# Block 0's groups in another order, its loads and stores moved, and the last block's quantised rows made by VectorE

## The chip, the cores and the metric

The kernel runs on the 8 cores of one Trainium2 chip. Each core computes 4 of the 32 sequences and shares nothing with the others. The time is the device time of the slowest core, in microseconds. Three runs of the kernel before took 1630.64, 1654.71 and 1867.44 us, so their median is 1654.71 us.

## What is computed

For each of 32 sequences of 2048 rows of 1024 numbers, one layer:

```
xn  = layernorm(x)
qkv = xn @ w_in.T                           # 1024 -> 3 x 1024, 16 heads of 64
o   = sliding window attention(q, k, v)     # blocks of 512 queries; each looks at its own
                                            # block and the one before, bias slope*distance
a   = o @ w_out.T
s   = max(max|xn| of the row, 1e-6) / 127   # the quantised branch
xq  = clip(round(xn / s), -128, 127)        # whole numbers
f   = (xq @ weight_q.T) * s * weight_scale + bias
out = x + a + f
```

## The kernel before

**Blocks, slots, steps.** A core handles 16 blocks of 512 rows (t = 0 to 15), four to a sequence; four row chunks (tc = 0 to 3) of 128 make a block. The program is unrolled in Python: for each block 8 slots (one per pair of heads) of 5 steps (one per tile of the attention matrix). A step is written (slot, i). In each step TensorE gets, in this order, the scores of one tile (L805, or L828 for slots 3 to 7), at most one *group* of 8 matmuls of 128x512 (L645, function `group`), and `pv`, probabilities times V, of earlier tiles (L897). The first block of a sequence has no previous block, so its slots have four tiles of 512, 384, 256 and 128 columns and an empty fifth step.

**The groups.** `K p` and `Q p` make keys and queries of head pair p, `V h tc` values of half h, `F tc h` is the quantised product, `P tc h` the output projection. `K+`, `Q+`, `V+` belong to the next block. `PLAN` says which group goes into which step; block 0 has its own table, `PLAN_0`, as it has no block before it whose F and P it could compute. The last block's remaining F and P follow in `LAST_SLOT` and `END_PLAN`. Groups write two PSUM banks (`dn`) in turn, so a group waits until the copy out of the group two before it is done.

**The chain of a slot.** When the last `pv` of a head pair is done, `den` (L910 to L913, ScalarE, three instructions) makes the reciprocal of the row sums at step 2 of the next slot (step 1 after an odd pair of 3 or more), `norm` (L920, L923, VectorE) multiplies at the step after it, and only then may `pv` of the next pair, at step 4, write the same two banks `oa` and `ob`. Masks (L881) are VectorE's too.

**Rows of x.** `xn_load`, `xn_stat`, `xn_norm`, `xn_amax` take the next block's rows: load by SyncE, statistics (L474 to L477) and maximum (L535) by VectorE, the rest by GpSimd; `xn_turn_dma` turns the four chunks by DMA (TN). They use two buffers `xpre`, so chunks 2 and 3 are loaded when chunks 0 and 1 are finished with. For block 1 the tables `SECOND_*` say at which steps of block 0 this happens.

**Quantised rows.** `xr_load` loads x again, `xq_make` quantises a chunk by six GpSimd instructions (L610, L614, L617, twice) into the single buffer `xq`, `xq_turn` turns it by DMA into one of two `xqfm`, `xq_bias` adds the bias to x on GpSimd (L628, four instructions), and `add_rows` (L737) adds that to u. For the last block `LAST_LOAD`, `LAST_MAKE`, `LAST_TURN` and `LAST_BIAS` give the steps.

**Weights.** They lie in DRAM as float32 and are cast by GpSimd's DMA queue. The K and Q weights of block 0 (numbers 0 to 15) come first and lie where `wq` and `wout` go later (`wq_sb`: 0 to 7, `wout_sb`: 8 to 15). Numbers 16 to 31 (block 1's) pass through four buffers `wqk` in turn and are stored as bf16 in DRAM (`w2bf`, by SyncE's queue, `store_wqk`); number n + 4 is loaded from float32 only after number n is stored. From number 32 on, SyncE loads them from `w2bf`. Each engine, and each of the two queues that issue DMAs (SyncE, GpSimd), works in the order written.

## Time and profile before

| | us |
|---|---|
| three runs | 1630.64, 1654.71, 1867.44 |
| the profiled execution, its own time | 1626.06 |
| its span on core 7, the slowest | 1624.4 |
| spans of the 8 cores | 1612.8 to 1624.4 |
| TensorE busy | 1576.1 (97%) |
| ScalarE, VectorE, GpSimd busy | 1058.5, 937.5, 840.8 |

The span runs from the first to the last instruction of a core, the profiled execution's own time is 1.66 us more. All times below are us from the span's start. In a row of a timeline "x8" counts merged instructions, and the bracket says how long the engine sat idle before the row and what released it.

### The profile page before, as it was taken

Reading aid. Unit: us, or ns where it says so; the run is one execution under the profiler, and the core shown is the slowest. Engines: PE = TensorE matmul, PEld = TensorE weight load, DVE = VectorE, ACT = ScalarE, POOL = GpSimd, SP = SyncE. Lnnn points to the kernel's source line nnn. Section 1 sums busy time; section 2 is a strip of 40 time slices with the busy share of each in tenths; the row PEclk is TensorE's granted clock in tenths of the full one; section 3 lists DMA queues with packets and bytes.
Section 4 is the critical chain, followed back from the end, with each engine's and each line's share of the span. In section 5 each row is a group of like instructions: output and inputs, shape, how many; then the busy total and the mean of one; then the engine's idle time right before and its main releaser. Section 6 shows DMA issues by size and latency. Waiting matters only on the chain.

```text
span 1624.4 us, 29492 instructions; the slowest of 8 cores (1612.8 to 1624.4 us)
## 1 busy us (share of the span) xinstructions
PE 1576.1 (97%) x8736; PEld 747.4 (46%) x8736; DVE 937.5 (58%) x1699; ACT 1058.5 (65%) x1966; POOL 840.8 (52%) x1258
## 2 busy tenths in 40 slices
PE   5788999999999999999999999999999999999997
PEld 2334444454444445444444544445444444544443
DVE  3644647556474665646556574655747566565453
ACT  4564776767656676776754667677675666767662
POOL 6325545535564564545546553464536645464275
PEclk9999999999999999999999999999999999999999
DMA  8948643635446353443535445343453634435232
GB/s 157 234 103 201 160 121 104 175 92 137 134 119 177 105 144 111 133 133 105 147 120 152 134 119 148 112 129 120 122 153 109 175 106 132 135 105 164 78 81 82
DMA packets 208705, 213.96 MB, mean 132 GB/s; under 512 B 139932, under 2 KB 140060, under 8 KB 208040
## 3 DMA queue, kind: packets, MB, share of 16 engines
q1 hardware_dynamic: 203368, 197.40, 42.9%
q0 software_dynamic: 5184, 14.68, 5.3%
q8 instruction: 76, 1.25, 0.3%
q14 instruction: 77, 0.63, 0.1%
HBM read 153.31 MB, written 37.75 MB: 118 GB/s over the span
## 4 chain that ended last, share of the span: by engine, by line
PE 88%; POOL 4%; DMA 4%; issue 1%; DVE 1%; ACT 1%; SPq 0%; POOLq 0%; DVEq 0%; ACTq 0%
PE dn L645 63%; PE oa L897 7%; PE ob L897 7%; PE sc L828 5%; PE sc L805 5%; DMA xqfm<-xq 1%; POOL xres L628 1%; DMA wv_sb<-wv 1%; DMA xpre<-x 1%; POOL u L737 1%; POOL xqt L610 1%; DMA xres<-x 1%; POOL xqt L614 1%; POOL xq L617 0%; POOL xpre L628 0%
## 5 line engine op out<-in xcount | busy, mean ns | idle before, releaser
L845 ACT ACTIVATE p<-sc,kbias_sb 128x512 bf16<-128x512 f32 (+3 forms) x1120 | 493.2, 535 | 270.8 <-PE sc L828 203.9
L645 PE MATMUL dn<-xnfm,wqk 128*128 128x512 bf16 x1920 | 447.3, 379 | 0.5 <-DMA xnfm<-xn 0.5
L737 POOL TENSOR_TENSOR u<-u,xres 128x256 f32<-128x256 f32 x240 | 170.6, 731 | 269.7 <-DVE u L754 243.2
L881 DVE TENSOR_TENSOR p<-p,tri_sb 128x512 bf16<-128x512 bf16 (+1 forms) x608 | 254.6, 420 | 91.9 <-ACT p L862 85.3
L645 PEld LDWEIGHTS dn<-xnfm,wqk 128*128 128x128 bf16 x1920 | 179.7, 98 | 218.1 <-issue 19.2
L862 ACT ACTIVATE p<-sc 128x1024 bf16<-128x1024 f32 (+3 forms) x228 | 218.0, 956 | 86.5 <-PE sc L805 85.8
L645 PE MATMUL dn<-wq_sb,xqfm 128*128 128x512 bf16 x1024 | 245.4, 383 | 10.5 <-DMA xqfm<-xq 8.2
L645 PE MATMUL dn<-wv_sb,xnfm 128*128 128x512 bf16 x1024 | 241.9, 379 | 2.4 <-DMA wv_sb<-wv 2.4
L645 PE MATMUL dn<-wout_sb,ofm 128*128 128x512 bf16 x1024 | 241.7, 380 | 0.0
L897 PE MATMUL oa<-p,vst 128*128 128x256 bf16 (+3 forms) x896 | 219.6, 300 | 9.7 <-DVE ofm L923 8.8
L897 PE MATMUL ob<-p,vst 128*128 128x256 bf16 (+3 forms) x896 | 217.6, 299 | 0.0
L722 DVE SCALAR_TENSOR_TENSOR u<-dn,small,wsb_sb 128x512 f32<-128x512 f32 x124 | 93.1, 751 | 158.5 <-PE dn L645 155.8
L478 POOL TENSOR_SCALAR small<-small 128x1 f32<-128x1 f32 x60 | 11.4, 190 | 312.6 <-DVE small L477 302.9
L628 POOL TENSOR_TENSOR xres<-xres,biasb_sb 128x256 f32<-128x256 f32 x248 | 167.0, 705 | 0.0
L754 DVE TENSOR_TENSOR u<-dn,u 128x512 f32<-128x512 f32 x124 | 85.7, 691 | 136.0 <-PE dn L645 131.0
L645 PEld LDWEIGHTS dn<-wq_sb,xqfm 128*128 128x128 bf16 x1024 | 97.8, 98 | 127.3 <-issue 22.7
L645 PEld LDWEIGHTS dn<-wv_sb,xnfm 128*128 128x128 bf16 x1024 | 100.0, 98 | 110.8 <-issue 4.0
L645 PEld LDWEIGHTS dn<-wout_sb,ofm 128*128 128x128 bf16 x1024 | 92.8, 98 | 119.7 <-issue 22.4
L920 DVE TENSOR_TENSOR ofm<-oa,r 64x512 bf16<-64x512 f32 x128 | 87.0, 680 | 98.7 <-ACT r L913 96.7
L897 PEld LDWEIGHTS oa<-p,vst 128*128 128x128 bf16 x896 | 87.8, 98 | 90.4 <-issue 11.6
L617 POOL TENSOR_SCALAR xq<-xqt 128x512 bf16<-128x512 f32 x128 | 79.7, 623 | 85.5 <-DMA xqfm<-xq 64.7
L910 ACT ACTIVATE r<-oa 64x512 f32<-64x512 f32 x128 | 76.1, 594 | 72.6 <-PE ob L897 70.0
(76 smaller groups left out, 1704.8 us busy)
## 6 DMA issues: line engine op xcount, KB each, us to landing
wqk<-w2bf SPq DMA_DIRECT2D x224, 256.0 KB, 2.9
xpre<-x SPq DMA_DIRECT2D x64, 512.0 KB, 4.4
xres<-x SPq DMA_DIRECT2D x64, 512.0 KB, 4.6
out<-u SPq DMA_DIRECT2D x124, 256.0 KB, 2.3
wqk<-w POOLq DMA_DIRECT2D x16, 256.0 KB, 6.9
w2bf<-wqk SPq DMA_DIRECT2D x16, 256.0 KB, 3.2
wq_sb<-w POOLq DMA_DIRECT2D x8, 256.0 KB, 11.2
wv_sb<-wv POOLq DMA_DIRECT2D x2, 1024.0 KB, 17.4
```

Of the source, the lines that this page charges most:

```text
L628: xb_ready[(t, tc)] = P.op("gpsimd", lambda e, cols=cols: e.tensor_tensor(out=buf[:, cols], in0=buf[:, cols], in1=biasb_sb[:, cols], op=AL ...
L645: tok = P.op("tensor", lambda e, k=k: e.matmul(out=dn[b][:, :], lhsT=lhs(k), rhs=rhs(k), start=(k == 0), stop=(k == n - 1)), waits=(waits ...
L722: v = P.op("vector", lambda e: e.scalar_tensor_tensor(out=u[:, :], in0=dn[b][:, :], scalar=xs[g][:, tc:tc + 1], in1=wsb_sb[:, cols], op0=A ...
L737: a = P.op("gpsimd", lambda e, q=q: e.tensor_tensor(out=u[:, 256 * q:256 * q + 256], in0=u[:, 256 * q:256 * q + 256], in1=buf[:, 512 * hal ...
L754: v = P.op("vector", lambda e: e.tensor_tensor(out=u[:, :], in0=dn[b][:, :], in1=u[:, :], op=ALU.add), waits=[tok, u_ready[(t, tc, half)]])
L805: tok = P.op("tensor", lambda e, h=h, slot=slot, tc=tc, c0=c0, c1=c1, hp=hp: e.matmul(out=sc[b % 2][:, 512 * hp + c0:512 * hp + c1], lhsT= ...
L828: tok = P.op("tensor", lambda e, r=r, slot=slot, tc=tc, c0=c0, c1=c1, hp=hp: e.matmul(out=sc[b % 2][:, 512 * hp + c0:512 * hp + c1], lhsT= ...
L845: tok = P.op("scalar", lambda e, c0=c0, c1=c1, hp=hp, o=o: e.activation(out=pbuf[b % NPB][:, 512 * hp + c0:512 * hp + c1], in_=sc[b % 2][: ...
L862: exp_done[b] = P.op("scalar", lambda e: e.activation(out=pt, in_=st, func=AF.Exp, scale=SCALE), waits=[sc_done[b]] + p_free[b % NPB])
L881: mask_done[b] = P.op("vector", lambda e: e.tensor_tensor(out=pt, in0=pt, in1=m, op=ALU.mult), waits=[exp_done[b], c_tok])
L897: end=end: e.matmul(out=bank[:, c0:c1], lhsT=vlhs(h, slot, tc), rhs=pbuf[bp % NPB][:, 512 * hp + c0:512 * hp + c1], start=(j == TILES[0]), ...
L920: P.op("vector", lambda e: e.tensor_tensor(out=dst[0:64, 512 * p:512 * (p + 1)], in0=oa[0:64, :], in1=r[0:64, :], op=ALU.mult), waits=[tok ...
```

## The change

It has three parts. **Block 0:** `PLAN_0` holds the same groups of slots 1 to 6 in other steps; chunks 2 and 3 of block 1's rows are loaded into `xres[1]` and `xres[2]` at steps (1, 0) and (1, 1), and their statistics, maxima and the turn come earlier; weights 2 and 3 are issued before the first rows' scalars and half 0 of V's weights one step sooner; `wq` is issued at (5, 1) instead of (3, 1) and waits for the turn of block 1's rows, `wout` at (7, 0) instead of (7, 2). **Stores:** numbers 16 to 19 are stored at (6, 0) of block 0, numbers 20 to 31 two at a time at step 2 of slots 0 to 5 of block 1; before, each K or Q group of number n issued the store of n + 2. **Last block:** `xq_make` is done by VectorE, four instructions to a chunk instead of six on GpSimd, from temporary tiles in `xn` into the free `xnfm`, and turned into `wv_sb`, whose weights are no longer needed; rows of chunks 2 and 3 are loaded into the other half of `wv_sb`, and load, make, turn and bias come earlier.

```diff
@@ -60,12 +60,12 @@
     [("V", 0, 1), ("V", 0, 2), ("V", 0, 3), None, None],
-    [("K", 2, 0), ("Q", 2, 0), ("V", 1, 0), None, None],
-    [("K", 3, 0), ("Q", 3, 0), ("V", 1, 1), None, None],
-    [("K", 4, 0), ("Q", 4, 0), ("V", 1, 2), None, None],
-    [("V", 1, 3), ("K", 5, 0), ("Q", 5, 0), None, None],
-    [("K", 6, 0), ("Q", 6, 0), None, None, None],
-    [("K", 7, 0), ("Q", 7, 0), None, None, None],
+    [None, ("K", 2, 0), ("Q", 2, 0), ("V", 1, 0), None],
+    [None, ("K", 3, 0), ("Q", 3, 0), ("V", 1, 1), None],
+    [("V", 1, 2), ("K", 4, 0), ("Q", 4, 0), ("V", 1, 3), None],
+    [None, ("K", 5, 0), ("Q", 5, 0), None, None],
+    [None, ("K", 6, 0), None, ("Q", 6, 0), None],
+    [None, ("K", 7, 0), ("Q", 7, 0), None, None],
     PLAN[7],
@@ -90,11 +90,10 @@
             (1, 4): ("P", 2, 1), (2, 0): ("P", 3, 0), (2, 1): ("P", 3, 1)}
-LAST_LOAD = {(0, 1): 0, (0, 2): 1, (5, 0): 2, (6, 3): 3}
-LAST_MAKE = {(4, 4): 0, (5, 3): 1, (6, 4): 2, (7, 2): 3}
-LAST_TURN = {(5, 2): 0, (6, 3): 1, (7, 2): 2, (7, 4): 3}
-LAST_BIAS = {(5, 2): 0, (6, 1): 1, (7, 1): 2}
-END_BIAS = (0, 0)
+LAST_LOAD = {(0, 1): 0, (0, 2): 1, (1, 3): 2, (1, 4): 3}
+LAST_MAKE = {(3, 4): 0, (4, 4): 1, (5, 4): 2, (6, 3): 3}
+LAST_TURN = {(4, 2): 0, (5, 2): 1, (6, 2): 2, (7, 1): 3}
+LAST_BIAS = {(4, 3): 0, (5, 2): 1, (6, 1): 2, (7, 1): 3}
@@ -103,10 +102,13 @@
 FIRST_SCALES = (1, 0)
-SECOND_LOAD = {(0, 3): 0, (0, 4): 1, (2, 3): 2, (3, 0): 3}
-SECOND_STAT = {(1, 4): 0, (2, 1): 1, (3, 3): 2, (4, 1): 3}
-SECOND_NORM = {(2, 0): 0, (2, 2): 1, (3, 4): 2, (4, 2): 3}
-SECOND_AMAX = {(2, 2): 0, (2, 4): 1, (4, 0): 2, (4, 4): 3}
+SECOND_LOAD = {(0, 3): 0, (0, 4): 1, (1, 0): 2, (1, 1): 3}
+SECOND_STAT = {(1, 4): 0, (2, 1): 1, (2, 4): 2, (3, 2): 3}
+SECOND_NORM = {(2, 0): 0, (2, 2): 1, (3, 0): 2, (3, 3): 3}
+SECOND_AMAX = {(2, 2): 0, (2, 4): 1, (3, 2): 2, (3, 4): 3}
+SECOND_TURN = (4, 1)
+
+STORE_STEP = 2
@@ -334,6 +336,7 @@
         wb_free = [[], []]
+        wv_free = [[], []]
         wqk_ready = {}
@@ -372,7 +375,9 @@
         def xsrc(t, tc):
-            return xpre[tc % 2] if t > 0 or tc < 2 else xres[tc - 2]
+            if tc < 2 or t > 1:
+                return xpre[tc % 2]
+            return xres[tc - 2 + t]
@@ -439,7 +444,7 @@
         g_half = P.op("gpsimd", lambda e: e.memset(mhalf[:, :], -0.5))
-        for seq in range(2):
+        for seq in range(4):
             load_first(seq, [xpre_ready[(0, 0)]])
@@ -456,7 +461,7 @@
         def load_wq():
-            late_w["wq"] = P.dma("gpsimd", wq_sb[:, :], wqh, "WQ", waits=wb_free[0])
+            late_w["wq"] = P.dma("gpsimd", wq_sb[:, :], wqh, "WQ", waits=wb_free[0] + xnfm_ready[1])
@@ -465,8 +470,11 @@
                 i = tc % 2
-                xpre_ready[(t, tc)] = P.dma("sync", xpre[i][:, :], xh[rows_of(t, tc), :], f"XP{i}",
-                                            waits=xpre_free[i])
+                if t == 1 and tc >= 2:
+                    sem, free = f"XR{tc - 1}", xres_free[tc - 1]
+                else:
+                    sem, free = f"XP{i}", xpre_free[i]
+                xpre_ready[(t, tc)] = P.dma("sync", xsrc(t, tc)[:, :], xh[rows_of(t, tc), :], sem, waits=free)
@@ -535,8 +543,8 @@
                 apply_absolute_value=True), waits=[stats[("d", t, tc)]])
-            if t == 0 and tc >= 2:
-                xres_free[tc - 2][:] = [tok, xn_ready[(t, tc)]]
+            if t <= 1 and tc >= 2:
+                xres_free[tc - 2 + t][:] = [tok, xn_ready[(t, tc)]]
             else:
@@ -594,16 +602,44 @@
-            if t == NT - 1 and tc < 2:
-                return xpre[tc], xpre_free[tc], f"XP{tc}"
-            i = (4 * t + (tc - 2 if t == NT - 1 else tc)) % NXR
+            if t == NT - 1:
+                if tc < 2:
+                    return xpre[tc], xpre_free[tc], f"XP{tc}"
+                return wv_sb[:, 2048 * (tc - 2):2048 * (tc - 1)].bitcast(F32), wv_free[0], f"XS{tc}"
+            i = (4 * t + tc) % NXR
             return xres[i], xres_free[i], f"XR{i}"
...
+        def xqfm_of(t, tc):
+
+            if t == NT - 1:
+                return wv_sb[:, 4096 + 1024 * tc:5120 + 1024 * tc], wv_free[1]
+            return xqfm[tc % 2][:, :], xqfm_free[tc % 2]
+
+        def xq_make_last(tc):
+
+            t = NT - 1
+            buf, g = xres_of(t, tc)[0], t % 3
+            for hf in range(2):
+                cols = slice(512 * hf, 512 * hf + 512)
+                tmp = xn[hf][:, :].bitcast(F32)
+                a = P.op("vector", lambda e, cols=cols, tmp=tmp: e.tensor_scalar(
+                    out=tmp, in0=buf[:, cols], scalar1=negm[g][:, tc:tc + 1],
+                    scalar2=alpha[g][:, tc:tc + 1], op0=ALU.add, op1=ALU.mult),
+                    waits=[xres_ready[(t, tc)], stats[("alpha", t)]] + xn_free[hf] + xnfm_free[NT % 2])
+                v = P.op("vector", lambda e, hf=hf, tmp=tmp: e.tensor_scalar(
+                    out=xnfm[NT % 2][:, 1024 * tc + 512 * hf:1024 * tc + 512 * hf + 512], in0=tmp,
+                    scalar1=MAGIC, scalar2=MAGIC, op0=ALU.add, op1=ALU.subtract), waits=[a])
+            xq_ready[(t, tc)] = v
+            stats[("taken", t, tc)] = a
+
         def xq_make(t, tc):
+            if t == NT - 1:
+                xq_make_last(tc)
+                return
             buf, g = xres_of(t, tc)[0], t % 3
@@ -630,9 +666,13 @@
         def xq_turn(t, tc):
-            dst = xqfm[tc % 2][:, :].rearrange("p (a b) -> p a b", a=8)
-            tok = P.turn(dst, xq[:, :], f"TQ{tc % 2}", [xq_ready[(t, tc)]] + xqfm_free[tc % 2])
-            xq_free[:] = [tok]
+            dst, free = xqfm_of(t, tc)
+            dst = dst.rearrange("p (a b) -> p a b", a=8)
+            src = xnfm[NT % 2][:, 1024 * tc:1024 * tc + 1024] if t == NT - 1 else xq[:, :]
+            tok = P.turn(dst, src, f"TL{tc}" if t == NT - 1 else f"TQ{tc % 2}",
+                         [xq_ready[(t, tc)]] + free)
+            if t < NT - 1:
+                xq_free[:] = [tok]
             xqfm_ready[(t, tc)] = tok
@@ -658,7 +698,6 @@
             xnfm_free[t % 2] = [tok]
-            store_wqk(seq + 2)
             if seq + 4 >= 32:
@@ -693,6 +732,7 @@
             xnfm_free[t % 2] = [tok]
+            wv_free[half][:] = [tok]
@@ -710,10 +750,12 @@
         def group_f(t, tc, half):
-            b, tok = group(8, lambda k: xqfm[tc % 2][:, 128 * k:128 * (k + 1)],
+            rows, free = xqfm_of(t, tc)
+            b, tok = group(8, lambda k: rows[:, 128 * k:128 * (k + 1)],
                            lambda k: wq_sb[:, 1024 * k + 512 * half:1024 * k + 512 * (half + 1)],
                            [xqfm_ready[(t, tc)], late_w["wq"]])
-            xqfm_free[tc % 2] = [tok]
+            if t < NT - 1:
+                free[:] = [tok]
             ui, u = u_of(t, tc, half)
@@ -970,7 +1012,7 @@
                         dense(t, LAST_SLOT[i] if t == NT - 1 and slot == 7 else (PLAN_0 if t == 0 else PLAN)[slot][i])
-                    if 0 < t + 1 < NT and at == XN_TURN_DMA:
+                    if 0 < t + 1 < NT and at == (SECOND_TURN if t == 0 else XN_TURN_DMA):
                         xn_turn_dma(t + 1)
@@ -988,12 +1030,11 @@
                     if t + 1 == 0:
+                        if at == (1, 3):
+                            load_wv0()
                         if at in FIRST_NORM:
...
                         if at == (1, 4):
-                            for seq in (2, 3):
-                                load_first(seq)
-                            load_wv0()
                             for seq in (4, 5):
@@ -1039,16 +1080,20 @@
                         xq_bias(t, LAST_BIAS[at])
-                    if t == NT and at == END_BIAS:
-                        xq_bias(t - 1, 3)
                     if t == 0 and at == (1, 0):
...
                             load_wqk(seq)
+                    if t == 0 and at == (6, 0):
+                        for seq in range(16, 20):
+                            store_wqk(seq)
+                    if t == 1 and slot < 6 and i == STORE_STEP:
+                        for seq in range(20 + 2 * slot, 22 + 2 * slot):
+                            store_wqk(seq)
                     if t == 0 and at == (2, 0):
                         load_late_constants()
-                    if t == 0 and at == (3, 1):
+                    if t == 0 and at == (5, 1):
                         load_wq()
-                    if t == 0 and at == (7, 2):
+                    if t == 0 and at == (7, 0):
                         load_wout()
```

How the order moves, first on TensorE in block 0. The piece of before begins with the second group of slot 1 (Q 2, step 1) and runs to slot 2's first scores (`sc`); `dn<-wv_sb` is V, `oa` and `ob` are `pv`.

```order
L645 MATMUL dn<-xnfm,wq_sb 128x512 x8
L805 MATMUL sc<-qa,ka 128x256
L805 MATMUL sc<-qb,kb 128x256
L645 MATMUL dn<-wv_sb,xnfm 128x512 x8
L805 MATMUL sc<-qa,ka 128x128
L805 MATMUL sc<-qb,kb 128x128
L897 MATMUL oa<-p,vst 128x512
L897 MATMUL ob<-p,vst 128x512
L897 MATMUL oa<-p,vst 128x384
L897 MATMUL ob<-p,vst 128x384
L805 MATMUL sc<-qa,ka 128x512
L805 MATMUL sc<-qb,kb 128x512
```

The change, from the first group of the same slot (K 2, now in step 1):

```order
L685 MATMUL dn<-xnfm,wq_sb 128x512 x8
L847 MATMUL sc<-qa,ka 128x256
L847 MATMUL sc<-qb,kb 128x256
L685 MATMUL dn<-xnfm,wq_sb 128x512 x8
L847 MATMUL sc<-qa,ka 128x128
L847 MATMUL sc<-qb,kb 128x128
L685 MATMUL dn<-wv_sb,xnfm 128x512 x8
L939 MATMUL oa<-p,vst 128x512
L939 MATMUL ob<-p,vst 128x512
L939 MATMUL oa<-p,vst 128x384
L939 MATMUL ob<-p,vst 128x384
L847 MATMUL sc<-qa,ka 128x512
```

K, Q and V each moved one step later: V now stands between the last scores of the slot and the `pv` that waits for `norm`, where no group stood, and none stands beside the scores of step 0.

SyncE's queue at the end of block 0, before. `WG0` to `WG3` are the loads of the four `wqk` buffers, from the turn of block 1's rows to the turn of block 0's first quantised chunk:

```order
L183 DMA_TRANSPOSE xnfm<-xn 128x8x128 [waits G] x2
L177 DMA w2bf<-wqk 128x1024 [waits WG0]
L177 DMA w2bf<-wqk 128x1024 [waits WG1]
L177 DMA w2bf<-wqk 128x1024 [waits WG2]
L177 DMA xres<-x 128x1024 [waits S]
L177 DMA w2bf<-wqk 128x1024 [waits WG3]
L177 DMA w2bf<-wqk 128x1024 [waits WG0]
L177 DMA w2bf<-wqk 128x1024 [waits WG1]
L183 DMA_TRANSPOSE xqfm<-xq 128x8x128 [waits G]
L177 DMA xres<-x 128x1024
```

The change, the same stretch:

```order
L185 DMA_TRANSPOSE xnfm<-xn 128x8x128 [waits G] x4
L179 DMA xres<-x 128x1024
L179 DMA w2bf<-wqk 128x1024 [waits WG0]
L179 DMA w2bf<-wqk 128x1024 [waits WG1]
L179 DMA w2bf<-wqk 128x1024 [waits WG2]
L179 DMA w2bf<-wqk 128x1024 [waits WG3]
L179 DMA xres<-x 128x1024 [waits V]
L185 DMA_TRANSPOSE xqfm<-xq 128x8x128 [waits G]
```

Two stores (numbers 20 and 21, the second `WG0` and `WG1`) no longer stand ahead of the turn `xqfm<-xq`, and the four others stand further from it.

VectorE in slot 3 of the last block, before (`u` is the copy out of an F or P group):

```order
L673 CAST k<-dn 128x512 [waits T]
L881 TENSOR_TENSOR p<-p,tri_sb 128x2x256 [waits S]
L673 CAST q<-dn 128x512 [waits T]
L881 TENSOR_TENSOR p<-p,tri_sb 128x2x128 [waits S]
L754 TENSOR_TENSOR u<-dn,u 128x512 [waits T,V]
L881 TENSOR_TENSOR p<-p,tri_sb 128x2x128 [waits S]
```

The change:

```order
L712 CAST k<-dn 128x512 [waits T]
L923 TENSOR_TENSOR p<-p,tri_sb 128x2x256 [waits S]
L629 TENSOR_SCALAR xn<-xpre,small 128x512 [waits XP0,TN]
L633 TENSOR_SCALAR xnfm<-xn 128x512 [waits V]
L629 TENSOR_SCALAR xn<-xpre,small 128x512
L633 TENSOR_SCALAR xnfm<-xn 128x512 [waits V]
L712 CAST q<-dn 128x512 [waits T]
L923 TENSOR_TENSOR p<-p,tri_sb 128x2x128 [waits S]
```

Four instructions (L629, L633, two halves) stand between a mask and the copy of Q out of PSUM; this happens in four slots. GpSimd's rows for them (24 in all) are gone.

## Rows read from the trace of the kernel before

**Rows 1.** The page, part 1: busy us, share of the span, instructions.
```profile
PE 1576.1 (97%) x8736; PEld 747.4 (46%) x8736; DVE 937.5 (58%) x1699; ACT 1058.5 (65%) x1966; POOL 840.8 (52%) x1258
```

**Rows 2.** Windows: length, busy of PE, PEld, DVE, ACT, POOL, clock, DMA, GB/s.
```profile
80.00:100.00 20.00, 14.52 (x64) 5.53 (x64) 9.70 (x21) 10.73 (x22) 1.49 (x2) 0.83 0.45 119
```

**Rows 3.** The chain that ended last, 0 to 165 us: start, us, what.
```profile
17.23 13.57 DMA wv_sb<-wv
...
114.87 17.51 DMA xqfm<-xq
```

**Rows 4.** Timeline of TensorE, block 0: start, us, line, operation, [idle before <- releaser].
```profile
31.18 1.89 PE L645 MATMUL dn<-wv_sb,xnfm 128*128 128x512 bf16 x8 [2.38 <-DMA wv_sb<-wv]
...
49.85 0.38 PE L897 MATMUL oa<-p,vst 128*128 128x512 bf16 x1 [2.19 <-DVE ofm L923]
...
51.04 3.48 PE L645 MATMUL dn<-xnfm,wq_sb 128*128 128x512 bf16 x8
...
60.71 0.38 PE L897 MATMUL oa<-p,vst 128*128 128x512 bf16 x1 [1.66 <-DVE ofm L923]
...
80.70 0.39 PE L828 MATMUL sc<-q,k 64*128 64x512 bf16 x2 [3.46 <-DVE q L673]
...
91.44 0.38 PE L897 MATMUL oa<-p,vst 128*128 128x512 bf16 x1 [3.36 <-DVE ofm L923]
...
93.24 3.02 PE L645 MATMUL dn<-xnfm,wout_sb 128*128 128x512 bf16 x8
...
100.35 0.39 PE L828 MATMUL sc<-q,k 64*128 64x512 bf16 x2 [1.76 <-ACT p L845]
...
101.44 1.89 PE L645 MATMUL dn<-xnfm,wqk 128*128 128x512 bf16 x8
```

**Rows 5.** Timeline of ScalarE and VectorE, block 0.
```profile
75.89 0.69 DVE L474 BATCH_NORM_STATS2 small<-xpre 128x6 f32<-128x512 f32 x1 [1.20 <-DMA xpre<-x]
...
86.07 1.78 ACT L845 ACTIVATE p<-sc,kbias_sb 128x384 bf16<-128x384 f32 x4 [3.08 <-PE sc L828]
...
87.88 0.59 ACT L910 ACTIVATE r<-oa 64x512 f32<-64x512 f32 x1
...
90.59 0.69 DVE L923 TENSOR_TENSOR ofm<-ob,r 64x512 bf16<-64x512 f32 x1
```

**Rows 6.** Timeline of TensorE, block 1.
```profile
119.16 1.89 PE L645 MATMUL dn<-xnfm,wqk 128*128 128x512 bf16 x8
...
132.93 3.57 PE L645 MATMUL dn<-wq_sb,xqfm 128*128 128x512 bf16 x8 [5.38 <-DMA xqfm<-xq]
```

**Rows 7.** Timeline of SyncE's queue and GpSimd, end of block 0.
```profile
85.12 29.66 SPq L177 DMA_DIRECT2D w2bf<-wqk  x3
...
108.79 0.62 POOL L617 TENSOR_SCALAR xq<-xqt 128x512 bf16<-128x512 f32 x1 [0.15 <-POOL xqt L614]
...
109.93 0.54 POOL L177 DMA_DIRECT2D wout_sb<-wout  x1
```

**Rows 8.** DMA issues, 0 to 170 us: count, KB each, us to landing.
```profile
wout_sb<-wout POOLq DMA_DIRECT2D x1, 2048.0 KB, 18.4
```

**Rows 9.** Timeline of TensorE, the end.
```profile
1592.24 1.89 PE L645 MATMUL dn<-wq_sb,xqfm 128*128 128x512 bf16 x8 [2.31 <-DVE p L881]
...
1600.80 5.29 PE L645 MATMUL dn<-wq_sb,xqfm 128*128 128x512 bf16 x16 [2.77 <-DMA xqfm<-xq]
...
1605.93 13.98 PE L645 MATMUL dn<-wout_sb,ofm 128*128 128x512 bf16 x64
```

**Rows 10.** Timeline of GpSimd and VectorE, the end.
```profile
1583.72 0.62 POOL L617 TENSOR_SCALAR xq<-xqt 128x512 bf16<-128x512 f32 x1 [2.28 <-DMA xqfm<-xq]
...
1590.80 0.75 DVE L722 SCALAR_TENSOR_TENSOR u<-dn,small,wsb_sb 128x512 f32<-128x512 f32 x1 [0.16 <-DMA out<-u]
```

**Rows 11.** Timeline of VectorE: two masks of one shape.
```profile
113.73 1.25 DVE L881 TENSOR_TENSOR p<-p,tri_sb 128x256 bf16<-128x256 bf16 x1 [2.38 <-ACT p L862]
...
121.88 0.42 DVE L881 TENSOR_TENSOR p<-p,tri_sb 128x512 bf16<-128x512 bf16 x1
```

2 lines of the change are left out of this document (1 added, 1 removed).

## The prediction

> **What bounds the kernel now.** I read the page's busy times first: TensorE works 1576.1 of 1624.4 us [rows 1], so it is the bound and a change can win only where it idles or runs slowly, 48 us in all. The page's slices put nearly all of that at the two ends. The engine's timeline says where. That of block 0, where a slot has only two or three groups, has six waits from 49.85 to 100.35: 2.19, 1.66, 1.63 (at 69.85, like the one before it and not shown), 3.46, 3.36 and 1.76, together 14.1 us [rows 4]. Four end at `norm`, one at the copy of Q 5, one at an exp. Ahead of them 2.38 us go to the first V weights. Three groups of 8 matmuls there last 3.48, 3.52 (at 81.79, not shown) and 3.02 us where 1.89 is normal (the row at 101.44): the windows row of 80 to 100 us has a granted clock of 0.83 [rows 2], so part of it ran at 1.2 instead of 2.4 GHz. Each such group comes behind one of the waits of 2.19 us or more; those of 1.66, 1.63 and 1.76 have none behind them. These three cost 1.6 + 1.6 + 1.1 = 4.3 us.
>
> In block 1 one wait is left: F 0 0 waits 5.38 us for its turned rows and then takes 3.57 us, 1.7 too long [rows 6]. SyncE's queue explains it: three stores held it from 85.12 to 114.78, because two of them wait for weights 20 and 21; only then, 5 us after the rows were made, was the turn issued, into the 2 MB load of `wout` that GpSimd had issued at 109.93 [rows 7]; it landed 17.51 us later [rows 3]. At the end [rows 9] TensorE waits 2.31 us for a bank, 2.77 us for the last turn, and 16 matmuls take 5.29 us instead of 3.5 (the row of 64 is 13.98, so 3.5 for 16). Behind both waits is GpSimd: its quantising waits 2.28 us for the buffer's turn, and the late copy out of F waits for a store of u that its queue had delayed [rows 10].
>
> **Block 0's order.** The count of groups stays, so TensorE's work does; only waits can change. Take the chain of slot 5: `den` starts at 87.88 and `norm` ends at 90.59 + 0.69 = 91.28, 3.4 us [rows 5]. Before, TensorE had K, Q and V in steps 0 to 2 and nothing beside `norm`. Now a slot of three groups has V (1.73 us, a 64-matmul row over 8) exactly there, and `pv` of the slot before comes one group sooner, so `den` may start sooner. For slots 1 to 3 I leave 0.4 us of waiting each, of 2.19 + 1.66 + 1.63. Slots 4 to 6 have two groups and nothing in step 3 except in slot 5. Counted from `pv`'s end: the exps of a tile or two (four instructions take 1.78, so 0.9 to 1.8) and the chain 3.4, less the two groups beside them, 3.5, leaves 0.8 to 1.7; with scores that must wait for their bank, I take 1.7 each. The wait for Q 5 was VectorE's: it stood at 75.89 for rows of x still landing [rows 5], behind which the copy of K 5 and `norm` queued. Those rows are now asked for some 20 us sooner, and the 2 MB of `wq` no longer compete. So the six waits fall from 14.1 to 1.2 + 5.0 = 6.2: **8 us won** (ends: 4, if the chain of each slot starts no sooner than now; 12, if nearly all close).
>
> **Clock in block 0.** With waits of 0.4 to 2 us I expect at most one slow group: 4.3 - 1.5, **3 us won** (0 to 4.3).
>
> **First V weights.** Before, the load was issued at 17.23 and took 13.57 us [rows 3]. Ahead of it now two issues less (0.54 each by the one of `wout` [rows 7]) and none of the last chunk's four scalars: 2.5 to 3 us sooner, with two weights out of its way. The scalars in turn slip a little, 0.2 us by my estimate. The wait of 2.38 goes: **2.2 us won** (0 to 2.4).
>
> **F 0 0.** Its turn has no store of numbers 20 and 21 ahead of it any more. K+ 0 was at 101.44 and F 0 0 due at 127.55; the quantised rows were ready at 108.79 + 0.62 = 109.4 [rows 7], so the turn is issued 18 us ahead of need, and even the 17.51 us of this time would do. **7.1 us won** (4 to 7.1). Late next could be weight 20: it stands in GpSimd's queue behind `wout`, now issued at the end of Q 7, 3.3 us before K+ 0. `wout` landed 18.4 us after its issue [rows 8], so 15.1 after K+ 0, weight 20 some 2 to 3 us later; it is due 119.16 - 101.44 = 17.7 us after K+ 0 [rows 4, 6]. So a wait of about **1 us** (0; 5 if `wq`, issued shortly before, still fills the queue, with 1.7 of slow clock).
>
> **The stores.** Twelve stores of 256 KB now come in pairs, each two steps before their buffer is loaded again. The loads they release are due 12 us and more later, so they cost nothing; the cover is that time, and without it a pair costs what the rival below says. Their bytes are the same.
>
> **The last block.** GpSimd loses 24 instructions of about 0.62 us [rows 10], 15 us, and no longer waits for one buffer. The bank comes free in time (2.31), the turn is ready (2.77), and the clock stays up (1.8). But P 0 0 needs `norm` of the last slot, which ends some 3.8 us after the last `pv`, the chain of 3.4 and its start; F 3 0 and F 3 1 fill 3.5, so 0.3 is left: **6.6 us won** (3 to 6.9). VectorE gains 16 `tensor_scalar` of 128x512. The trace has none of that size there. Bounds: 0.42, a bf16 mask of 128x512 [rows 11], and 0.75, the copy out of F [rows 10]; the operands are float32, but the pair reads one tensor, so I take 0.55. Four come in a row, 2.2 us, between a mask and the copy of Q. The copy is needed only two groups later (over 3.5 us), so the cover is the second bank and the masks' lead; I charge **1 us** in all (0 to 8). The upper end has its reason in a row: a mask of 128x256 took 1.25 us at 113.73, while GpSimd was adding, though twice the columns take 0.42 [rows 11]. If each of the four waits that long behind a bias or an add of GpSimd, a burst lasts 5 us.
>
> The Trainium skill (SBUF — State Buffer, Who interferes with whom) has a rule that speaks against moving this work: VectorE's two-input SBUF instructions and its 2-port modes share a port pair with GpSimd, and whoever comes second blocks fully. The slow mask agrees. By that rule, with every one of the 16 held up, the last block's term would be the upper end; without it, nothing.
>
> **Sum.** 8 + 3 + 2.2 + 7.1 - 1 + 6.6 - 1 = 24.9 us. The profiled execution took 1626.06, so 1601 us. The profile is 4.6 us under the lowest run shown (1630.64) and 29 under the median of the three, 1654.71, which the other two runs pull up; I put the time where most runs should be, **1603**.
>
> **The rivals.**
>
> *The chain keeps block 0* (0.20). A slot's waits only change places: ScalarE takes exps before `den`, and with two groups a slot is as long as its chain. For: the slot of K 6 and Q 6 already waited with only two groups. Against: in slots 1 to 3 TensorE idled exactly where V now stands. Then block 0 gives 4 + 0 instead of 8 + 3, and the time is 1603 + 7 = 1610.
>
> *VectorE becomes the hold-up of the last block* (0.12). Bursts of 5 us, as above, delay copies and masks four times by about 2 us: 1603 + 7, and if weight 20 is late as well, 1616. This is also the port rule's case. Against: VectorE is 58% busy and GpSimd has 15 us less to do.
>
> *Nearly all idle time goes* (0.16). Waits 12, clock 4.3, V 2.4, F 7.1, end 6.9 give 32.7, to 1593.
>
> *Slower than before* (0.04). Block 1's weights starve. A store stands behind everything that SyncE waits for; that queue has been held 29.66 us by three rows before [rows 7]. GpSimd then cannot reload its buffer and everything behind stands still, the quantising too. It decides from the point where a pair is held over 12 us. Held 17 us in each of the six slots, TensorE would wait 5 us and run slowly for 1.7, six times: 40 us, 1603 + 40 = 1643. Against it: no row ahead of these stores waits for anything that far off.
>
> *The forecast* (0.48). Everything above within a few us.
>
> **Numbers.** 1603. The range takes in the bounds: 1590 below; above, the two middle rivals and a run as far over the profile as those shown can be, 1630. Two per cent, about what a measurement of this kernel can tell from no change, is 32.5 us. Faster by more needs the third rival or an uneven pair of runs: 0.24. Within: 0.72. Slower: 0.04.
>
> **What would show it.** Right: `pv`'s waits for `norm` in block 0 at most 2 us each; K+ 0 at about 88 instead of 101.44; V's first group without a wait; no wait for `xqfm` anywhere; the last block's GpSimd share well down, and 64 matmuls of P starting some 4 us after the last `pv`. Wrong: waits of 2.5 us and over in slots 4 to 6 with groups of 3 us behind them; a wait of K 2 of block 1 for `wqk`; `tensor_scalar` rows of a microsecond and copies of Q that end late; new waits in block 1's slots. A run in which block 0 saves under 6 us would make the sum wrong by its largest term.

## The result: 1.2% faster, with 4 of the 11 us forecast for block 0

The changed kernel took 1608.47 us (median of 4 runs, 1607.27 to 1609.71). The kernel before took 1642.68 (median of 4 runs, 1626.28 to 1867.44). The ratios in this document leave out the disturbed runs, in which the cores of one die or both run at a lower granted clock; they are why the medians stand further apart. The ratio is 0.9884, with an interval of 0.9870 to 0.9898: faster by 1.2%, so under the 2% that count as a change here. The forecast was 1603 us, with 1590 to 1630 as its range. Its own sum said 24.9 us off the profiled execution's 1626.06; the new profiled execution took 1608.58, so 17.5 us went.

The page's busy times, to be read beside [rows 1]. TensorE's 1557.0 can't be compared to the us, since 167 of its matmul records are missing from this trace (8569 of 8736); idle times of 0.16 us "<-issue" are such holes.

```profile
PE 1557.0 (97%) x8569; PEld 746.1 (46%) x8736; DVE 949.3 (59%) x1715; ACT 1058.6 (66%) x1966; POOL 824.8 (51%) x1234
```

GpSimd has 24 instructions and 16.0 us less, VectorE 16 instructions and 11.8 us more.

Where the time went shows best if TensorE's timeline is cut at five instructions that both kernels have. In this table every figure is the mean over the eight cores, in us:

| stretch of TensorE's timeline | before | after | forecast |
|---|---|---|---|
| start to the first V group | 29.96 | 29.57 | -2.2 |
| first V group to K+ 0 | 67.26 | 63.28 | -11 |
| K+ 0 to the first `pv` behind F 0 0 | 35.15 | 28.62 | -6.1 |
| from there to the last `pv` | 1461.37 | 1459.76 | } -5.6 |
| last `pv` to P's 64 matmuls | 8.00 | 4.98 | } |
| P and the rest | 18.50 | 18.72 | 0 |
| span | 1620.25 | 1604.92 | -24.9 |

The mean span fell by 15.3 us, the slowest core's by 17.4 (1624.4 to 1607.0): the cores also lie closer together now, 1602.4 to 1607.0 instead of 1612.8 to 1624.4. I had read the stretches from core 7 of before, the slowest one. The fourth row also shows how far two mean spans can differ without a cause in the edit: in the runs below that change block 0 or its loads and stores (1, 3, 4, 6, 7, 8, 11, 12) it lies between 1458.2 and 1460.3.

TensorE's timeline in block 0 and the start of block 1, core 0, to be read against [rows 4, 6]: start, us, what, and in the bracket the idle time before it and its releaser.

```profile
46.00 0.38 PE L939 MATMUL oa<-p,vst 128*128 128x512 bf16 x1 [0.53 <-DVE ofm L965]
...
55.26 0.38 PE L939 MATMUL oa<-p,vst 128*128 128x512 bf16 x1 [1.34 <-DVE ofm L965]
...
66.53 0.38 PE L939 MATMUL oa<-p,vst 128*128 128x512 bf16 x1 [1.93 <-DVE ofm L965]
...
68.47 3.26 PE L685 MATMUL dn<-xnfm,wout_sb 128*128 128x512 bf16 x8
...
75.03 0.39 PE L870 MATMUL sc<-q,k 64*128 64x512 bf16 x2 [1.18 <-DVE q L712]
...
82.58 0.38 PE L939 MATMUL oa<-p,vst 128*128 128x512 bf16 x1 [1.00 <-DVE ofm L965]
...
90.95 0.39 PE L870 MATMUL sc<-q,k 64*128 64x512 bf16 x2 [2.32 <-DVE q L712]
...
92.35 3.27 PE L685 MATMUL dn<-xnfm,wqk 128*128 128x512 bf16 x8
...
119.88 1.89 PE L685 MATMUL dn<-wq_sb,xqfm 128*128 128x512 bf16 x8
```

The reader is to see three things. Three of the four waits for `norm` have shrunk, from 2.19, 1.66 and 3.36 to 0.53, 1.34 and 1.00; the third has grown from 1.63 to 1.93. The waits for a copy of Q have grown: 1.18 and 2.32 (2.4 and 2.32 on six of the eight cores) where there was one, of 3.46 on core 7 and 2.2 on core 0. And K+ 0 starts at 92.35 instead of the forecast 88 and is itself a slow group of 3.27; on the mean of the cores it went from 97.2 to 92.8. F 0 0 at 119.88 waits for nothing and lasts 1.89.

The granted clock of 80 to 100 us, 0.83 in [rows 2], is now 0.91 in the same window; core 0 of before had 0.83 there too (length, busy of PE, PEld, DVE, ACT, POOL, clock, DMA share, GB/s):

```profile
80.00:100.00 20.00, 16.41 (x79) 6.65 (x80) 8.87 (x20) 11.97 (x25) 3.75 (x6) 0.91 0.71 174
```

The end, TensorE's timeline, against [rows 9]:

```profile
1582.96 0.81 PE L939 MATMUL ob<-p,vst 128*128 128x384 bf16 x3
1583.61 3.62 PE L685 MATMUL dn<-wq_sb,wv_sb 128*128 128x512 bf16 x16
1588.26 13.97 PE L685 MATMUL dn<-wout_sb,ofm 128*128 128x512 bf16 x63 [1.04 <-DVE xn L764]
```

There is no wait for a bank and none for a turn, and 16 matmuls take 3.62 us instead of 5.29. The wait of 1.04, the same on all cores, ends at the copy of an F group out of PSUM. VectorE's rows that stand in GpSimd's place are shown in the last section.

### The profile page after: what moved, and what is told of

It is laid out like the page before. It is cut to its first block, busy times and chain, and to the rows that moved or that the text cites. A ratio compares the mean times of both kernels' runs of the same rounds, so it can differ in the third digit from the quotient of the medians.

```text
span 1607.0 us, 29298 instructions; the slowest of 8 cores (1602.4 to 1607.0 us)
## 1 busy us (share of the span) xinstructions
PE 1557.0 (97%) x8569; PEld 746.1 (46%) x8736; DVE 949.3 (59%) x1715; ACT 1058.6 (66%) x1966; POOL 824.8 (51%) x1234
## 4 chain that ended last, share of the span: by engine, by line
PE 89%; POOL 3%; issue 2%; DVE 1%; SPq 1%; DMA 1%; ACT 1%; POOLq 0%; DVEq 0%; ACTq 0%
PE dn L685 64%; PE ob L939 7%; PE oa L939 7%; PE sc L847 6%; PE sc L870 6%; SPq L185 1%; DMA xnfm<-xn 1%; POOL xres L664 1%; POOL u L779 1%; DMA xpre<-x 0%; DVE ofm L965 0%; POOL xqt L646 0%; ACT p L887 0%; SPq L179 0%; POOL xqt L650 0%
## 5 line engine op out<-in xcount | busy, mean ns | idle before, releaser
L923 DVE TENSOR_TENSOR p<-p,tri_sb 128x512 bf16<-128x512 bf16 (+1 forms) x608 | 258.2, 426 | 91.6 <-ACT p L904 81.5
L685 PE MATMUL dn<-wout_sb,ofm 128*128 128x512 bf16 x975 | 232.7, 380 | 7.4 <-issue 5.7
L685 PE MATMUL dn<-wq_sb,xqfm 128*128 128x512 bf16 x938 | 223.9, 379 | 2.2 <-issue 1.6
L939 PE MATMUL oa<-p,vst 128*128 128x384 bf16 (+3 forms) x881 | 214.1, 298 | 5.7 <-DVE ofm L965 4.8
L664 POOL TENSOR_TENSOR xres<-xres,biasb_sb 128x256 f32<-128x256 f32 x240 | 162.6, 709 | 0.0
L685 PEld LDWEIGHTS dn<-wq_sb,xqfm 128*128 128x128 bf16 x960 | 91.2, 98 | 106.8 <-issue 6.7
L870 PE MATMUL sc<-q,k 64*128 64x512 bf16 (+3 forms) x1120 | 112.5, 300 | 4.2 <-DVE q L712 3.5
L952 ACT ACTIVATE r<-oa 64x512 f32<-64x512 f32 x128 | 76.1, 594 | 61.4 <-PE ob L939 58.8
```

The source lines that it names most:

```text
L664: xb_ready[(t, tc)] = P.op("gpsimd", lambda e, cols=cols: e.tensor_tensor(out=buf[:, cols], in0=buf[:, cols], in1=biasb_sb[:, cols], op=AL ...
L685: tok = P.op("tensor", lambda e, k=k: e.matmul(out=dn[b][:, :], lhsT=lhs(k), rhs=rhs(k), start=(k == 0), stop=(k == n - 1)), waits=(waits ...
L870: tok = P.op("tensor", lambda e, r=r, slot=slot, tc=tc, c0=c0, c1=c1, hp=hp: e.matmul(out=sc[b % 2][:, 512 * hp + c0:512 * hp + c1], lhsT= ...
L923: mask_done[b] = P.op("vector", lambda e: e.tensor_tensor(out=pt, in0=pt, in1=m, op=ALU.mult), waits=[exp_done[b], c_tok])
L939: end=end: e.matmul(out=bank[:, c0:c1], lhsT=vlhs(h, slot, tc), rhs=pbuf[bp % NPB][:, 512 * hp + c0:512 * hp + c1], start=(j == TILES[0]), ...
```

## The experiments

All are edits of the changed kernel if nothing else is said. "Stretch" is the mean over the cores from the first V group to K+ 0. Spans by core come from the profiled execution.

**1. The old order of block 0's groups.**

```diff
-    [None, ("K", 2, 0), ("Q", 2, 0), ("V", 1, 0), None],
+    [("K", 2, 0), ("Q", 2, 0), ("V", 1, 0), None, None],
...
```

> The changed kernel (ratio 0.988 to the kernel before) with block 0's groups in their old steps; loads, stores, statistics and the last block stay changed. Theory A (the chain of a slot bounds block 0, and the new order of groups hides a part of it): `pv` waits for `norm` again 1.6 to 2.2 us in slots 1 to 3, and the time from the first V group to K+ 0 of block 1, 63.3 us on the mean of 8 cores now and 67.3 before, comes to 67 or more; the ratio to before rises by 0.004 to 0.007, to 0.992 to 0.995. Theory B (block 0's gain came from the rows of x that land sooner, not from the order): the stretch stays at 63 to 64 us and the ratio at 0.988 to 0.990.

Ratio 0.9934 (0.9911 to 0.9957), as theory A has it. The stretch is 71.2 us against 63.3: the order wins 7.9 us here. But 71.2 is also 4.0 more than in the kernel before, which has this same order. In these stretches TensorE's mean idle time is 14.4 us (before 13.9, changed 10.5), its busy time for the same work 56.8 (53.3, 52.8), at a granted clock of 0.89 (0.95, 0.97). So half of the 7.9 is clock: behind waits of up to 3.4 us the groups ran partly at 1.2 GHz. The third wait for `norm` is 3.2 us here, twice that of before (1.63): the order is old, but the row statistics now stand ahead of it (run 6).

**2. The last block undone.** Rows quantised by GpSimd again, with the old steps:

```diff
-LAST_LOAD = {(0, 1): 0, (0, 2): 1, (1, 3): 2, (1, 4): 3}
-LAST_MAKE = {(3, 4): 0, (4, 4): 1, (5, 4): 2, (6, 3): 3}
+LAST_LOAD = {(0, 1): 0, (0, 2): 1, (5, 0): 2, (6, 3): 3}
+LAST_MAKE = {(4, 4): 0, (5, 3): 1, (6, 4): 2, (7, 2): 3}
...
```

> The changed kernel with the last block as it was: rows quantised by GpSimd at the old steps, one buffer xq, two xqfm. Theory A (GpSimd's quantising and its single buffer held up the end): the waits of some 2.3 us behind the last block's copies out of F and of 2.8 us for the last turn come back with a slow pair of groups; the time between the last `pv` and the first P group goes from 5.0 to 8 us on the mean of the cores, and the ratio rises by 0.003, to 0.991 to 0.992. Theory B (the bursts on VectorE cost as much as they save, the masks and copies they delay stall TensorE): no more than 0.001, 0.988 to 0.989.

Ratio 0.9927 (0.9912 to 0.9943). The mean span is 5.8 us longer, 2.8 of it between the last `pv` and P, where the wait for the last turn is back (2.8 us on seven cores), and 2.9 ahead of it, where the wait for a bank is back (1.7 to 2.5 us). The rest of the 2.9 is no more than that row's spread. Theory A holds; the forecast had 5.6 for this part.

**3. The old stores, `wq` and `wout`.** The stores of numbers 16 to 31 at the groups again, `wq` at (3, 1) without waiting for the turn of block 1's rows, `wout` at (7, 2):

```diff
+            store_wqk(seq + 2)
...
-                    if t == 0 and at == (5, 1):
+                    if t == 0 and at == (3, 1):
                         load_wq()
-                    if t == 0 and at == (7, 0):
+                    if t == 0 and at == (7, 2):
                         load_wout()
```

> The changed kernel with the stores issued by each K or Q group for the weights two ahead, wq issued at (3, 1) and wout at (7, 2), as before. Theory A (two stores ahead of the turn, and wout beside it, made F 0 0 wait): F 0 0 waits 4 to 6 us again and its group runs slowly, block 1's F 0 0 to K+ 0 distance goes from 28.5 back to some 35 us on the mean of the cores; ratio 0.992 to 0.993. Theory B (the turn is in time anyway since block 0 is shorter and the rows are ready): 0.988 to 0.989.

Ratio 1.0013 (0.9998 to 1.0029): all of the gain is gone. The stretch is 72.5 us, and the next one 35.3 as before: K+ 0 waits for its turned rows (up to 13.6 us) and F 0 0 for its own (2.6 to 6.3 us). The second is what theory A has; the first, which neither theory has, makes the loss more than twice as large as expected, and the kernel before has no such wait on any core. Three things are undone at once here; runs 7, 8 and 9 take them one by one.

**4. The old first weights.**

```diff
-        for seq in range(4):
+        for seq in range(2):
             load_first(seq, [xpre_ready[(0, 0)]])
...
```

> The changed kernel with the first weights issued as before: two ahead of the first rows' scalars, weights 2 and 3 and the first half of V's after them. Theory A (the two extra issues on GpSimd delay the first chunk's scalars by 1.5 us, which takes back most of what the earlier V weights give): first turn at 11.5 us instead of 13.0 and first K group at 19.6 instead of 20.5, but V's first group waits again 1.5 to 2.5 us and starts at 30 instead of 29.6; the ratio moves by less than 0.0005. Theory B (the first rows' delay is hidden behind the loads and the earlier V weights are worth 2.2 us): V's first group at 31.5 or later, ratio 0.0014 higher, 0.9898.

There is no ratio for this kernel; its two undisturbed runs took 1610.36 and 1612.35, and the spans are 1601.6 to 1608.7, mean 1604.81 against 1604.92. The first V group comes at 30.25 instead of 29.57, but the first transposes start at 11.66 instead of 13.04. By the mean span alone this part of the change would be worth nothing, but that difference is within the spread named above. Over all profiled kernels of this document the start of the first V group, as a mean over the cores, says more: with the first weights as changed it lies at 28.96 to 29.57 us (ten kernels, mean 29.2), with the old ones at 29.96 to 30.25 (the kernel before, runs 4 and 5, mean 30.2). So this part is worth about 1 us, and the changed kernel's own 29.57 is the latest of its ten. Theory A put the wait at 1.5 to 2.5 us; it is 1.3 on the mean and none to 2.6 by core.

**5. The kernel before with the new order alone.**

```diff
@@ kernel before @@
-    [("K", 2, 0), ("Q", 2, 0), ("V", 1, 0), None, None],
+    [None, ("K", 2, 0), ("Q", 2, 0), ("V", 1, 0), None],
...
```

> The kernel before with the new order of block 0's groups and nothing else. From the first V group to K+ 0 the kernel before takes 67.3 us on the mean of the cores, the changed kernel 63.3, the changed kernel with the old order 71.2. Theory A (the order is worth about 8 us wherever it stands, and the statistics of block 1's rows, moved earlier, cost block 0 about 4): this stretch takes 59 to 60 us, less than in the changed kernel, and the kernel is about 8 us below the kernel before, 0.995. Theory B (order and statistics only work together: the order pays because the rows come early and VectorE no longer waits for their load): the stretch takes 65 to 67 us, 0 to 2 us won, ratio 0.999. F 0 0 should wait 5 us or so in either case, since the stores are as before.

Ratio 0.9974 (0.9963 to 0.9985). The stretch is 63.9 us, 3.4 under the kernel before: between the theories, and nearer to B. The waits of TensorE on core 0 (engine, operation, what it waited for: us in total, times, longest) show what is left ahead of K+ 0, and that it is not what is left in the changed kernel; behind it F 0 0 waits 2.5 to 6.9 us, as both theories have it:

```profile
PE sc L828 <- DVE q L673: 5.8, 2, 3.4
PE dn L645 <- DMA wv_sb<-wv: 3.1, 1, 3.1
PE oa L897 <- DVE ofm L923: 3.1, 4, 1.3
```

The changed kernel, core 0:

```profile
PE oa L939 <- DVE ofm L965: 4.8, 4, 1.9
PE sc L870 <- DVE q L712: 3.5, 2, 2.3
```

With the rows of x late, VectorE stands for them and the copy of Q is late; with the rows early, their statistics run sooner, and `norm` is.

**6. The statistics behind `norm`.**

```diff
-SECOND_STAT = {(1, 4): 0, (2, 1): 1, (2, 4): 2, (3, 2): 3}
-SECOND_NORM = {(2, 0): 0, (2, 2): 1, (3, 0): 2, (3, 3): 3}
-SECOND_AMAX = {(2, 2): 0, (2, 4): 1, (3, 2): 2, (3, 4): 3}
+SECOND_STAT = {(1, 4): 0, (2, 0): 1, (2, 4): 2, (3, 0): 3}
+SECOND_NORM = {(2, 0): 0, (2, 2): 1, (3, 0): 2, (3, 2): 3}
+SECOND_AMAX = {(2, 3): 0, (3, 3): 1, (3, 4): 2, (4, 3): 3}
```

> The changed kernel; the statistics and the maxima of block 1's rows stand at other steps of block 0, none at steps 1 and 2, so that none lies ahead of the copy of Q and of norm. Theory A (VectorE's order in slots 2 and 3 lengthens the chain of a slot): the waits of pv for norm in slots 2 and 3, 1.34 and 1.93 us on core 0, fall under 0.7 together with the slow group behind them, the stretch from V to K+ 0 falls from 63.3 to 60 to 61.5, and the time is 2 to 3 us under that of the changed kernel. Theory B (the chain is den and ScalarE's exps; VectorE has slack): the stretch stays at 63 to 64. If the turn of block 1's rows then comes too late, K+ 0 would wait for xnfm, which neither expects: it is needed 14 us after the last row is made.

Ratio 0.9872 (0.9856 to 0.9888). The stretch falls from 63.3 to 61.3, the mean span from 1604.9 to 1601.6. VectorE's timeline of the changed kernel in slot 3 has the place:

```profile
60.98 0.69 DVE L712 CAST k<-dn 128x512 bf16<-128x512 f32 x1 [1.62 <-PE dn L685]
61.58 0.28 DVE L923 TENSOR_TENSOR p<-p,tri_sb 128x256 bf16<-128x256 bf16 x1
61.78 0.69 DVE L482 BATCH_NORM_STATS2 small<-xres 128x6 f32<-128x512 f32 x1
62.39 0.67 DVE L484 BATCH_NORM_STATS2 small<-xres 128x6 f32<-128x512 f32 x1
63.16 0.21 DVE L485 BATCH_NORM_AGGREGATE small<-small 128x2 f32<-128x12 f32 x1
63.29 1.19 DVE L543 TENSOR_REDUCE small<-xres 128x1 f32<-128x1024 f32 x1
64.40 0.68 DVE L712 CAST q<-dn 128x512 bf16<-128x512 f32 x1
65.00 0.67 DVE L962 TENSOR_TENSOR ofm<-oa,r 64x512 bf16<-64x512 f32 x1
65.69 0.69 DVE L965 TENSOR_TENSOR ofm<-ob,r 64x512 bf16<-64x512 f32 x1
```

Four instructions, 2.6 us, ahead of the copy of Q and `norm`; `norm` ends at 66.38 and TensorE's `pv` at 66.53 has waited 1.93. In the experiment the same place reads:

```profile
61.76 0.69 DVE L712 CAST q<-dn 128x512 bf16<-128x512 f32 x1 [0.84 <-PE dn L685]
62.37 0.67 DVE L962 TENSOR_TENSOR ofm<-oa,r 64x512 bf16<-64x512 f32 x1
63.05 0.69 DVE L965 TENSOR_TENSOR ofm<-ob,r 64x512 bf16<-64x512 f32 x1
```

and the `pv` behind it waits 0.24. On all cores the waits for `norm` in slots 1 to 3 are now 0.53, 0.40 and 0.25. The mean idle time in the stretch falls by 2.4 us (10.5 to 8.1), while the busy time grows by 0.4, at a granted clock of 0.96. Theory A holds.

**7. The old stores alone.** `store_wqk(seq + 2)` in the groups again; `wq` and `wout` as changed.

> The changed kernel with the stores of weights 16 to 31 where the kernel before has them; wq and wout stay at their new steps. Theory A (the stores alone made F 0 0 wait, as they held SyncE's queue ahead of the turn): F 0 0 waits 4 to 7 us, K+ 0 is not late, and the time is 5 to 8 us over the changed kernel. Theory B (it was the loads of wq and wout that filled the queues): F 0 0 does not wait and the time is that of the changed kernel within 1 us.

Ratio 0.9889 (0.9872 to 0.9907), that of the changed kernel. Theory A, that the stores alone made F 0 0 wait, falls. SyncE's and GpSimd's queues on core 0 (the `w2bf` row is read as in [rows 7]):

```profile
72.73 34.09 SPq L179 DMA_DIRECT2D w2bf<-wqk  x3
106.92 1.51 SPq L185 DMA_TRANSPOSE xqfm<-xq  x1
...
89.00 0.53 POOL L179 DMA_DIRECT2D wout_sb<-wout  x1 [16.45 <-PE dn L685]
```

The stores hold the queue even longer than before, 34.09 us, and the turn is issued at 106.92, 5.3 us later than in the changed kernel (101.67). But `wout`, issued at 89.00, had landed at 102.70 and no longer competes: GpSimd's next quantising, which waits for this turn, starts at 112.53, so the turn took at most 5.6 us and F 0 0 at 119.60 waits for nothing. On every core `wout` lands before this turn is issued, and the turn takes 4.5 to 6.0 us.

**8. `wq` early.**

```diff
-            ... "WQ", waits=wb_free[0] + xnfm_ready[1])
+            ... "WQ", waits=wb_free[0])
...
-                    if t == 0 and at == (5, 1):
+                    if t == 0 and at == (3, 1):
                         load_wq()
```

> The changed kernel with the load of wq two slots earlier and not waiting for the turn of block 1's rows; stores and wout as changed. Theory A (the turn and the 2 MB load must not be in flight together; the turn starves): K+ 0 waits for xnfm on most cores, up to 14 us, the stretch from V to K+ 0 is 70 to 73 us instead of 63.3, and F 0 0 does not wait. Theory B (the starving in the kernel with all of that undone came from its stores): the stretch stays at 63 to 64 and the time is that of the changed kernel.

Ratio 0.9957 (0.9912 to 1.0002), the stretch 72.4 us, K+ 0 anywhere from 95.8 to 110.3 on the cores. The queue of core 7, with `wq` issued at 61.01, and TensorE:

```profile
51.46 48.72 SPq L185 DMA_TRANSPOSE xnfm<-xn  x4
...
103.83 3.57 PE L685 MATMUL dn<-xnfm,wqk 128*128 128x512 bf16 x8 [11.70 <-DMA xnfm<-xn]
```

The same four turns occupy the queue for this long in the changed kernel on the same core:

```profile
52.76 18.69 SPq L185 DMA_TRANSPOSE xnfm<-xn  x4
```

Theory A holds as to the time: `wq` must not be loaded here while these turns are in flight. The load is slow too, 39.4 us to its landing. But the kernel before has this load at the same step and beside its own turns, and neither is slow (last section), so it is not simply that the two are in flight together. Theory A has nothing of what comes behind K+ 0: four cores also wait 1.7 to 4.4 us for the weights of block 1 (`wqk`), and from K+ 0 to the `pv` behind F 0 0 it takes 32.8 us instead of 28.6. F 0 0 waits nowhere.

**9. `wout` late.**

```diff
-                    if t == 0 and at == (7, 0):
+                    if t == 0 and at == (7, 2):
                         load_wout()
```

> The changed kernel with the load of wout issued two steps later, at (7, 2) as in the kernel before; its stores and wq stay changed. The old stores alone, with wout early, gave no wait of F 0 0. Theory A (F 0 0 waits when its turn is in flight together with the 2 MB of wout, whichever engine is the cause of that): wout is issued behind weight 20 at about 97 to 103 us, the turn at 101.7 takes 13 to 17 us instead of the 5 to 7 of the changed kernel and lands at 115 to 119, and F 0 0, due at 119.9, waits 0 to 2 us; some core waits. Theory B (only a turn issued late, behind the held stores, makes F 0 0 wait): the turn lands as in the changed kernel and nothing moves. Both put the time within 2 us of the changed kernel, so the landing of the turn tells them apart, not the time.

The interval is too wide to use (0.968 to 1.007); spans by core are 1605.8 to 1613.0, mean 1608.8, 3.9 over the changed kernel. `wout` is issued 0.5 us behind F 0 0's turn here and lands at 119 to 123. That turn takes 8.9 to 13.4 us from issue to landing on the eight cores, no more than in the changed kernel (9.6 to 16.2; the 5 to 7 that the expectation gives for it is not what the trace has), and F 0 0 waits for it nowhere. It is the second chunk's turn that is slow, 10.6 to 15.4 us instead of 3.1 to 4.4. So theory A fails on the turn that it speaks of. What comes late instead is rows of x for block 2: VectorE stands 6.55 us for them on core 0, and the copy out of an F group, queued behind their statistics, makes TensorE wait, by 2.8 to 4.2 us on the eight cores.

```profile
123.43 0.69 DVE L482 BATCH_NORM_STATS2 small<-xpre 128x6 f32<-128x512 f32 x1 [6.55 <-DMA xpre<-x]
...
125.06 0.75 DVE L764 SCALAR_TENSOR_TENSOR u<-dn,small,wsb_sb 128x512 f32<-128x512 f32 x1
```

```profile
125.96 1.89 PE L685 MATMUL dn<-xnfm,wqk 128*128 128x512 bf16 x8 [2.80 <-DVE u L764]
```

Neither theory had this wait. It makes up nearly the whole loss, 3.7 of the 3.9 us on the mean.

**10. VectorE's quantising twice over.**

```diff
-            for hf in range(2):
+            for hf in (0, 1, 0, 1):
```

> The changed kernel; the last block's rows are quantised twice over by VectorE, the same values to the same places, eight instructions to a chunk in place of four. Theory A (the work lies in VectorE's slack): bursts of 4 to 6.5 us instead of 2.0 to 3.3, and still at most 1 us more in all. Theory B (the slack is one burst deep, as the copy of Q is needed two groups, 3.5 us, later): each of the four bursts then makes TensorE wait 0.5 to 3 us for q or for the second bank, 2 to 10 us in all between 1515 and 1583 us.

The time of the profiled execution is 1613.92, the mean span 1610.2, 5.3 over the changed kernel (the interval against the kernel before, 0.968 to 1.006, is of no use). Two of the four bursts reach TensorE on every core, each with more than 1.9 us, and on three cores, as on core 0, a slow group stands behind the first:

```profile
1547.43 3.34 PE L685 MATMUL dn<-wq_sb,xqfm 128*128 128x512 bf16 x8 [2.11 <-DVE q L712]
...
1573.46 1.89 PE L685 MATMUL dn<-wq_sb,wv_sb 128*128 128x512 bf16 x8 [1.92 <-DVE u L764]
```

Theory B, though only for two bursts of the four: VectorE's slack is between one burst (2.0 to 3.3 us, no wait) and two.

**11. Further steps from the changed kernel.** Run 6, and:

```diff
-    [None, ("K", 5, 0), ("Q", 5, 0), None, None],
+    [("K", 5, 0), ("Q", 5, 0), None, None, None],
...
-    [None, ("K", 7, 0), ("Q", 7, 0), None, None],
+    [("K", 7, 0), ("Q", 7, 0), None, None, None],
```

with the first weights 2 and 3 issued behind the scalars of the first and second chunk.

> The changed kernel with the statistics behind norm (that alone took the stretch from V to K+ 0 from 63.3 to 61.3 us) and two steps more. K and Q of slots 4 and 6 stand at steps 0 and 1 instead of 1 and 2, so that the copy of Q comes before norm. Theory A: the two waits for the copy of Q, 2.25 and 2.33 us, turn into waits of pv for norm of 0.5 to 1.5, and the stretch falls to 59 to 60.5. Theory B (the chain of den and norm sets the slot): waits only change their name and the stretch stays at 61 to 62. And weights 2 and 3 are issued behind the scalars of the first and of the second chunk, half 0 of V behind those of the third: the first turn at 11.7 to 12.2 us instead of 13.0, the first V group at 28.5 to 29.3. Time: Theory A 1601 to 1604, B 1604 to 1606.

Ratio 0.9813 (0.9684 to 0.9941), the lowest run 1600.93, spans 1597.1 to 1599.3. The stretch is 58.8 us, even under theory A's 59 to 60.5. The first transposes do start at 11.55, but the first V group only at 29.52, within the 28.96 to 29.57 of the changed order: the step wins nothing beyond that order.

**12. The same without the step on the first weights.**

> The changed kernel with the statistics behind norm, and K and Q of slots 4 and 6 at steps 0 and 1; the first weights and half 0 of V are issued as in the changed kernel. The kernel of the run before this had both, and another order of the first weights: its stretch from V to K+ 0 was 58.8 us on the mean of the cores (63.3 in the changed kernel), its first V group at 29.5 (29.6), its spans 1597.1 to 1599.3. Theory A (all it won lies in block 0's slots; the order of the first weights is worth nothing): the stretch is 58.5 to 59.2, the first V group at 29.0 to 29.6, the spans are 1596 to 1600, and the time is 6 to 7 us under the changed kernel, a ratio of 0.984 to 0.986 to the kernel before. Theory B (part of it was the earlier first turn): the spans are 1 to 2 us longer than that.

Ratio 0.9834 (0.9800 to 0.9869), five undisturbed runs from 1600.58 to 1604.01, all below the changed kernel's lowest of 1607.27, though taken at another time. The stretch is 58.8 us, the first V group comes at 29.00, the spans are 1595.8 to 1599.9, their mean 7.0 us lower than the changed kernel's: theory A. Of the 7.0, 4.5 are the stretch; the rest lies in other stretches, within their spread. This is the best version. TensorE's waits on core 0:

```profile
PE sc L870 <- ACT p L887: 3.5, 2, 1.8
PE oa L939 <- DVE ofm L965: 1.8, 4, 0.7
```

The copy of Q is out of the list; what is late next is ScalarE's exp, twice 1.8 us.

## Why the prediction was right in part, step by step

**Block 0's order, 8 us, and its clock, 3 us: wrong; this is the step that failed.** Together 4.0 us came instead of 11. That is the prediction's own sign of a wrong largest term, block 0 saving under 6 us. Mean idle time in the stretch fell from 13.9 to 10.5 us, where I had 14.1 to 6.2 for the six long waits, and busy time by 0.6. Three things made it so.

The first is VectorE's order around `norm`, which the sum of waits in slots 1 to 3 left out: it had 0.4 us each, 1.2 together, and 0.53, 1.34 and 1.93 came, 3.8 together. The prediction took `norm` as starting when `den` is done and put V beside it. But the change also moved row statistics and maxima to steps 1 and 2 of slots 2 and 3, ahead of the copy of Q and `norm`, and the prediction looked at these rows only for the load that they wait for. Putting them behind `norm` gave 2.0 us (run 6), and the three waits then were 0.53, 0.40 and 0.25, the forecast's 1.2.

The second is the wait for a copy of Q. I gave it wholly to VectorE standing for rows of x [rows 5], and let it vanish. In slots 4 and 6 `norm` comes at step 2, just when Q's matmuls end, and the copy of Q stands behind it. VectorE's timeline of the changed kernel, core 0, slot 6, where Q's matmuls end at 88.63 and TensorE waits until 90.95:

```profile
88.37 0.68 DVE L962 TENSOR_TENSOR ofm<-oa,r 64x512 bf16<-64x512 f32 x1 [1.23 <-ACT r L955]
89.07 0.69 DVE L965 TENSOR_TENSOR ofm<-ob,r 64x512 bf16<-64x512 f32 x1
89.79 0.29 DVE L923 TENSOR_TENSOR p<-p,tri_sb 128x256 bf16<-128x256 bf16 x1
90.12 0.69 DVE L712 CAST q<-dn 128x512 bf16<-128x512 f32 x1
```

So early rows did not end that wait. In the sum this mistake hardly shows: it had 5.0 us for slots 4 to 6, all of it waits for `norm`, and 5.1 came on the mean, 4.4 of it for Q. The size was luck. K and Q one step sooner ended the wait, for another 2.4 us (61.25 in run 6 to 58.81 in run 12). With both, the stretch is 8.4 us shorter than before, of the 11 forecast. That K+ 0 then starts at 87.8 on the mean of the cores is not the prediction's 88 come true: that was counted down from core 7's 101.44, and the mean began at 97.2.

The third is the base. The three slow groups and the wait of 3.46 are core 7's, whose stretch was 70.3 us; on the other seven it was 65.4 to 67.5, and they waited 2.2 to 2.6 us for Q. On the mean the six waits were 12.9 us and not 14.1. A clock term of 3 us could not be had from a mean whose busy time is only 1.3 over that of run 12 (53.3 against 52.0). Nor does core 7's pattern, a slow group behind each wait of 2.19 us or more and behind none of the shorter ones, hold on the others: before, K+ 0 took 3.4 to 3.6 us behind the wait of 1.76 on four cores, and in the changed kernel the wait of 2.32 is on all eight and K+ 0 is slow on four. What else decides it stays open.

The rival "the chain keeps block 0" had 4 and nothing for the clock, and 1610: that is the size measured. Its reason, exps before `den`, was not what held in the changed kernel, where `norm` and the copies of Q end the waits and exps end a wait of 0.6 us at most; a wait of 1.76 us for exps is there in the old order (before, run 1) and again in runs 11 and 12, when VectorE is out of the way.

What of the 4.0 us belongs to the order can't be said by itself, since order and tables act together: in the surroundings of before it gives 3.4 (run 5), in the new ones 7.9 (run 1). The rest of the change without the order makes this stretch 4.0 longer than before (run 1), nearly all of it as clock.

**First V weights, 2.2: too much, 0.4 by the table and about 1 by all runs (run 4).** The wait did go, but 2.38 was core 7's: the mean over the cores was 1.2, and three cores had none. A part of it went into the start. GpSimd issues two more loads before the first chunk's scalars (2.36 us for four issues), so the first transposes start at 13.04 instead of 11.55 and the first K group at 20.48 instead of 19.57. I had allowed 0.2 for that.

**F 0 0, 7.1 less 1: right, but it was not the stores alone.** 6.5 us came, and no wait for weight 20. As predicted, the turn is issued 18.2 us ahead of need, on every core, and so has time for its 9.6 to 16.2 us, though `wout` is still in flight beside it at first. But this early issue is not needed: with the stores back (run 7) the turn is issued 5 to 10 us later and there is no loss, since `wout` has landed and the turn takes 4.5 to 6.0 us. Nor does the late `wout` alone bring the wait back (run 9), as the turn is then still issued early enough. The wait is there where stores and `wout` are both late (before, runs 3 and 5; 15.5 to 19.4 us for the turn in the kernel before). All three also have the early `wq`; that late stores and late `wout` are enough by themselves was not run.

**The stores, 0: right.** Run 7 equals the changed kernel: pairs cost nothing and win nothing. The slower rival, block 1's weights starving, did not occur in the changed kernel; four cores of run 8 waited 1.7 to 4.4 us for them.

**The last block, 6.6 less 1: right.** 4.6 us by the table, 5.8 by undoing it (run 2). P's 64 matmuls start 4.98 us after the last `pv`; "some 4" was said. VectorE's bursts cost nothing rather than 1, and run 10 shows that one more burst each would have cost 5. The rival by which VectorE holds up the last block, and with it the port rule's case, did not occur.

**The sum**: 9.6 us too much on the mean of the cores, 7.0 of it in block 0, 1.8 in the first weights, 1.0 and 0.2 at the end, less 0.4 at F 0 0. That the time, 1608, still lies within 6 us of the 1603 is owed to the 2 us that I had added to the sum and to the slowest core, which won 2 us more than the mean.

## What to carry to other kernels

When work is put beside a chain, list for each engine of the chain what stands ahead of it in program order, in the changed kernel and at every slot, and price those instructions too; what moves for another reason (here row statistics moved because their load came early) may land exactly there. Take the base of a sum from the mean of the cores and look at the slowest beside it: here core 7 had 4.2 us more of waits and slow clock than the mean. And when a transfer is late, look both at when it is issued and at what is in flight beside it, and undo one at a time: here removing either cause was enough.

## What the runs showed of the hardware

Four DMA transposes and a 2 MB load cast by GpSimd's queue held each other up in one run and not in another. The transposes are the turns of 128x1024 (`xnfm`), the load is `wq`; all figures are core 7's. With no `wq` in flight the four turns took 18.69 us of SyncE's queue (the changed kernel). In run 8 the first turn was issued at 51.46 and the load at 61.01: the turns took 48.72 and the load landed after 39.4 us. In the kernel before the load came first, and the turns took no longer than without it, while the load landed after 18.4 us:

```profile
61.39 0.62 POOL L177 DMA_DIRECT2D wq_sb<-wq  x1
...
64.21 18.73 SPq L183 DMA_TRANSPOSE xnfm<-xn  x4
```

So being in flight together is not enough. Whether the order of issue makes the difference no run here tests. In the bad case the DMA engines were not idle, but moved little. The windows are run 8 from 60 to 100 us, the changed kernel from 52 to 72, and the kernel before from 61 to 81; the last two columns are DMA share and GB/s.

```profile
60.00:100.00 40.00, 24.44 (x122) 9.71 (x120) 19.44 (x40) 20.57 (x42) 4.80 (x7) 0.86 1.31 87
```

```profile
52.00:72.00 20.00, 16.48 (x89) 6.88 (x87) 16.68 (x27) 11.32 (x22) 10.26 (x16) 1.00 1.20 168
```

```profile
61.00:81.00 20.00, 14.91 (x82) 6.17 (x80) 13.26 (x26) 11.66 (x24) 7.10 (x12) 1.00 1.12 259
```

VectorE's float32 `tensor_scalar` of 128x512, which the trace of before did not have, took 0.54 us (0.43 for the one that writes bf16), near my 0.55. Beside GpSimd's additions it took 0.89 and 0.70. VectorE's timeline of the changed kernel, a burst alone and one during GpSimd's bias:

```profile
1529.76 0.54 DVE L629 TENSOR_SCALAR xn<-xpre,small 128x512 f32<-128x512 f32 x1
1530.41 0.43 DVE L633 TENSOR_SCALAR xnfm<-xn 128x512 bf16<-128x512 f32 x1
...
1542.42 0.89 DVE L629 TENSOR_SCALAR xn<-xpre,small 128x512 f32<-128x512 f32 x1
1543.41 0.70 DVE L633 TENSOR_SCALAR xnfm<-xn 128x512 bf16<-128x512 f32 x1
```

GpSimd's side of the second, four bias additions of 128x256, and four such additions with VectorE at other work (other sets of four took up to 2.78):

```profile
1542.17 3.27 POOL L664 TENSOR_TENSOR xres<-xres,biasb_sb 128x256 f32<-128x256 f32 x4
...
1560.47 2.55 POOL L664 TENSOR_TENSOR wv_sb<-wv_sb,biasb_sb 128x256 f32<-128x256 f32 x4
```

Both engines are slower, by 0.27 to 0.35 us an instruction on VectorE and 0.12 to 0.18 on GpSimd, and neither stops for the length of the other's instruction each time (0.64 or more for GpSimd's, 0.43 or more for VectorE's): one after the other the burst and the four additions would take 2.0 + 2.55 us, and both were done in 3.6, from 1542.17 to 1545.73. The Trainium skill (SBUF — State Buffer, Who interferes with whom) has whoever comes second block fully until the other's instruction ends. If these instructions fall under that rule, it cost a burst 1.3 us here (3.3 instead of 2.0) where the prediction's upper end had 2.8 (5 instead of 2.2), and none of it reached TensorE.
